# A graph network on one core: another form of the segment maximum, and the dense node blocks dealt to other stages

## The chip, the core and the metric

The kernel runs on one core of a Trainium2 chip. The time is device microseconds (us) of that core for one execution, median of several runs. The core has a matrix engine (TensorE, PE in the profile; its weight loads are PEld), a vector engine (VectorE, DVE), a scalar engine for functions of one input (ScalarE, ACT), a general engine (GpSimd, POOL) which here issues the indirect DMAs (gathers and scatters of rows by an index list), and SyncE (SP), which issues the plain DMAs. Each engine runs its own program in order; they meet at semaphores.

## The reference

100,000 nodes with 64 features, 25,000 edges sorted by their target `dst`. Four graph layers follow each other, each as `x = layernorm(x + layer(x))`. Cut to what matters:

```python
# layer 0
logits  = w1[target] - w2[source] + d            # per edge, 64 channels
seg_max = segment_max(logits, target)
e       = exp(logits - seg_max[target])
a       = e / segment_sum(e, target)[target]
out     = segment_sum(a * (w3[source] + d), target)
# layer 1: mean of neighbours, two products, batch norm, relu, row normalisation
# layer 2: attention with one head (leaky relu, segment softmax)
# layer 3: three graph convolutions, the last one into a softmax
h = relu(conv(x, W1, b1)); h = relu(conv(h, W2, b2)); h = conv(h, W3, b3)
x = layernorm(x + softmax(h, axis=1))
```

A node that is no edge's target gets nothing from segment sums, so its row goes through all four layers alone ("dense" work). Rows of nodes with edges are computed apart and written over the dense ones at the end.

## The kernel before

Edges are handled in 25 steps (`ITERS`) of two chunks (b = 0, 1) of 512 edges. A chunk lies with 64 or 128 channels on the partitions and 512 edges along the free axis, so that sums and maxima over the edges of one target are scans along that axis: `k.same` holds 1 where an edge has the target of the edge before it. The program is a row of stages, each with a barrier at its end: index work; an edge network; the first attention (`attention_stage`); the mean layer; batch norm; the update; the dense stage; the second attention; the convolutions `gcn1_stage`, `gcn2_stage`; the output stage. Tiles are named by stage (`at_`, `me_`, `up_`, `de_`, `g_` for both convolutions, `ou_`).

**The dense work** is cut into 97 blocks of 1024 nodes (8 nodes on each of 128 partitions) and a last one of the same size that overlaps (98 blocks). `DenseLane` holds the instructions of a block, as three parts that are pipelined: x (batch norm product up to `dve_norm2`), y (the three products of layer 3, `pe_turn3` to `pe_zback`) and z (softmax and layer norm, `dve_max` to `dve_norm4`, then a store to `out`). A stage that takes blocks along runs, at edge step q, part x of its block q, part y of block q-1 and part z of block q-2 between its own instructions; `LaneOrder` holds that order. The order on each engine is written by hand in the function `step` of each engine's block. 23 blocks lie in gcn1, 22 in gcn2, 23 in the output stage and 30 in the dense stage, where two lanes run side by side (15 pairs).

**The first attention** needs the running maximum of the logits over the edges of a target. ACT makes `anew` (0 where the edge continues its target, -1e30 where it starts a new one). DVE scans with state = max(state + anew, logit) into M (L1215), and later makes L = logit - M (L1239), A = M of the edge before + anew (L1240) and A = A - M (L1243): the exponents of the edge's weight and of the decay of the running sum. ACT takes their exponentials (L1149, L1140), and DVE's next step scans the sums (L1180, L1184). In the same ACT program, between them, stand `act_flat` (L931) and the squares of the finished rows, L1137, on which DVE's L1247 waits.

**Gathers** are issued by POOL in `gather_loop` (L1346): eight indirect DMAs of 128 rows a step (sixteen in the first attention), and a copy of the next index columns (L1331, L450). W has two buffers, so POOL may be two steps ahead of the transposes that free them.

**The output stage** has two parts. In 25 steps it gathers, scans and keeps the third convolution of all edges in `G3` in SBUF, with 23 blocks beside it. Then each engine runs `finish` 25 times: softmax, residual and layer norm of one step's edges (DVE L3352 to L3383, ACT L3288 to L3298), into a buffer F, and POOL scatters F into `out` with eight indirect DMAs a step (`scatter`, L3117). The scatter waits (`beside.stored`) until all blocks are stored, since it writes over their rows. F has two buffers; L3383 waits until the scatter of two steps before has landed. The loads of the residual rows (`rest`, X3) are issued by SP after all block loads.

## Time and profile before

| | us |
|---|---|
| median of 3 runs (3369.0 to 3388.23) | 3370.6 |
| profiled execution, its own time | 3347.96 |
| span of the profiled execution | 3346.2 |
| first attention, 240 to 876 | 636 |
| gcn1, 1962 to 2330 | 368 |
| gcn2, 2332 to 2757 | 425 |
| output stage, steps with gathers, 2759 to 3062 | 303 |
| output stage, finish and scatter, 3062 to 3346 | 284 |

The page gives each engine's busy time over the whole span; since the stages have different limits, the shares of the stages decide. The PEclk slices are tenths of TensorE's full clock; the last three of the forty are 5, with PE idle. "Idle before" of a row names what ended the wait of the instruction.

### The profile page before, as it was taken

To read this page: it belongs to the slowest core of one execution; us is meant where nothing else is said; L and a number is where in the kernel's file an instruction comes from. 1 tells how busy PE (TensorE), PEld (TensorE's weight loads), DVE (VectorE), ACT (ScalarE), POOL (GpSimd) and SP (SyncE) were. 2 spreads that over 40 slices of the span, in tenths; PEclk is the share of its full clock that TensorE was granted. 3 is DMA by queue.
4 is the path that set the end of the run, shared out by engine and by line. 5 is a ranking of instruction groups with operands and counts; after the bars stand their busy time and mean duration, and the time that the engine had idled before them with its cause. 6 is when DMAs were issued, how large, how long until landed. Compare 5 with 4: busy or idle time off the path is not lost. (4 is left out here: it accounts for less than half of the span.)

```text
span 3346.2 us, 53978 instructions
## 1 busy us (share of the span) xinstructions
PE 2459.9 (74%) x14171; PEld 1675.7 (50%) x14171; DVE 2486.4 (74%) x4558; ACT 1724.2 (52%) x3950; POOL 1925.5 (58%) x1870
## 2 busy tenths in 40 slices
PE   3976666666578789979946779998999998995000
PEld 1543444444467667745525556665666656663000
DVE  5569999999777758859966747776566665888553
ACT  3784444444222258858841126665566655775221
POOL 4008888887488800068870047775655437886776
PEclk9988787787777888879977989998999998997555
DMA  4133333433466668733313445555445543332111
GB/s 129 64 96 87 107 99 107 109 106 98 119 199 196 191 144 180 153 104 115 112 46 75 113 127 167 157 162 159 135 136 141 139 106 108 112 114 68 47 47 27
DMA packets 742887, 393.28 MB, mean 118 GB/s; under 512 B 517090, under 2 KB 649265, under 8 KB 742770
## 3 DMA queue, kind: packets, MB, share of 16 engines
q1 hardware_dynamic: 691582, 333.94, 36.4%
q0 software_dynamic: 51200, 58.03, 6.8%
q8 instruction: 54, 0.88, 0.1%
q14 instruction: 51, 0.42, 0.0%
HBM read 217.18 MB, written 175.64 MB: 117 GB/s over the span
## 5 line engine op out<-in xcount | busy, mean ns | idle before, releaser
L1341 POOL DMA_INDIRECT g_W<-t,g_cols x400 | 463.2, 1158 | 260.8 <-PE g_pS L2901 116.4
L460 POOL DMA_INDIRECT fr_W<-in_x,fr_idx x400 | 496.0, 1240 | 127.6 <-issue 107.7
L1341 POOL DMA_INDIRECT me_W<-t,me_cols x200 | 236.0, 1180 | 58.0 <-issue 46.9
L1341 POOL DMA_INDIRECT ou_W<-t,ou_cols x200 | 222.6, 1113 | 58.1 <-issue 40.8
L3433 POOL DMA_INDIRECT de_V<-t,de_cols x200 | 215.8, 1079 | 53.6 <-issue 41.4
L3117 POOL DMA_INDIRECT out<-ou_F,ou_ways x200 | 200.1, 1000 | 77.5 <-issue 53.3
L1058 PE MATMUL at_pL<-at_XF,w_logit 128*128 128x512 f32 x100 | 89.7, 996 | 123.0 <-ACT at_XF L1105 123.0
L1331 POOL COPY g_cols<-pos 128x8 int32 (+1 forms) x50 | 19.8, 396 | 241.2 <-POOLq L85 241.0
L1331 POOL COPY de_cols<-pos 128x8 int32 (+1 forms) x25 | 8.1, 324 | 261.4 <-POOLq L85 261.2
L931 ACT ACTIVATE me_nzt<-me_pXT 128x512 f32<-128x512 f32 x47 | 28.1, 598 | 170.9 <-PE me_pXT L914 170.9
L914 PE MATMUL at_pXT<-ident,at_nz 128*128 128x128 f32 x200 | 40.3, 336 | 93.8 <-ACT at_nzt L931 52.3
L1887 DVE TENSOR_TENSOR_SCAN me_S<-same,me_S,me_pA 64x512 f32<-64x512 f32 (+1 forms) x50 | 63.6, 1271 | 58.9 <-issue 40.1
L1058 PEld LDWEIGHTS at_pL<-at_XF,w_logit 128*128 128x128 f32 x100 | 28.3, 313 | 154.4 <-ACT at_XF L1105 129.6
L450 POOL COPY fr_idx<-src 128x8 int32 (+1 forms) x25 | 6.9, 278 | 160.1 <-POOLq L85 159.8
L3383 DVE TENSOR_TENSOR ou_F<-ou_O,ou_st 128x256 f32<-128x256 f32 x50 | 21.1, 425 | 96.8 <-DMA out<-ou_F,ou_ways 83.0
L3288 ACT ACTIVATE ou_O<-ou_O 128x256 f32<-128x256 f32 x50 | 18.8, 418 | 142.4 <-DVE ou_O L3359 142.4
L1490 DVE TENSOR_TENSOR g_T<-g_pY,g_st 128x512 f32<-128x512 f32 x45 | 30.8, 684 | 82.3 <-PE g_pY L1471 82.3
L1563 PE MATMUL g_pH<-g_H,w 128*128 128x512 f32 x180 | 88.1, 612 | 0.0
L2444 ACT ACTIVATE a_QY<-a_pB 128x512 f32<-128x512 f32 x25 | 14.9, 598 | 140.1 <-PE a_pB L2421 140.1
L3030 DVE TENSOR_TENSOR_SCAN g_S<-same,g_S,g_WF 128x512 f32<-128x512 f32 (+1 forms) x50 | 64.3, 1286 | 28.8 <-ACT g_WF L2961 28.8
L2419 PE MATMUL a_pB<-center,a_S 64*128 64x64 f32 x400 | 56.1, 281 | 38.5 <-DVE a_S L2546 38.3
L2116 PE MATMUL up_pU<-center,up_U 128*128 128x128 f32 x400 | 66.8, 336 | 15.5 <-DVE up_st L2222 15.5
(619 smaller groups left out, 8536.8 us busy)
## 6 DMA issues: line engine op xcount, KB each, us to landing
mg_y<-wanted SPq DMA_DIRECT2D x50, 256.0 KB
at_nx<-in_x SPq DMA_DIRECT2D x50, 256.0 KB, 2.6
x<-at_nz SPq DMA_DIRECT2D x50, 256.0 KB, 3.3
x1T<-at_nzt SPq DMA_DIRECT2D x50, 256.0 KB, 2.9
t<-up_X SPq DMA_DIRECT2D x100, 128.0 KB, 2.0
t<-g_HS SPq DMA_DIRECT2D x50, 256.0 KB
t<-g_HD SPq DMA_DIRECT2D x50, 256.0 KB, 3.4
g_D<-t SPq DMA_DIRECT2D x50, 256.0 KB
```

Of the source, the lines that this page charges most:

```text
L460: self.nc.gpsimd.indirect_dma_start(out=self.W[w][b][:, (2 * t + h) * C:(2 * t + h + 1) * C], out_offset=None, in_=self.table, in_offset=b ...
L914: s = self.nc.tensor.transpose(self.pXT[:, n * P:n * P + P], self.Z[b][:, n * (P + 1):n * (P + 1) + P], self.k.ident[:, :])
L1058: t.matmul(pL[b][:, :], k.w_logit[:, :], XF[b][:, :], start=True, stop=False, skip_group_check=True)
L1341: nc.gpsimd.indirect_dma_start(out=slot(w, b, t), out_offset=None, in_=table, in_offset=bass.IndirectOffsetOnAxis(ap=cols[w][:, c:c + 1], ...
L1490: self.nc.vector.tensor_tensor(groups(self.T[:, :], G), groups(self.pY[:, :], G), over(self.st[:, 1, :], C), ALU.mult).then_inc(e["scaled" ...
L1563: s = self.nc.tensor.matmul(self.pH[:, h, :], self.k.w2[:, :], self.H1[:, h, :], start=True, stop=True)
L1887: v.tensor_tensor_scan(S[b][:, :], k.same[0:C, at], pA[b][:, :], S[1 - b][:, CE - 1:CE], ALU.mult, ALU.add).then_inc(e["summed"], 1)
L2116: i = t.matmul(pU[x % 2][b][:, n * P:n * P + P], U[x % 2][b][:, n * P:n * P + P], k.center[:, :], start=True, stop=True)
L2419: t.matmul(pB[w][:, m:m + C], S[b][:, n * P:n * P + P], k.center[0:C, 0:C], start=b == 0 and n == 0, stop=False, skip_group_check=True)
L3030: v.tensor_tensor_scan(S[b][:, :], k.same[:, at], WF[b][:, :], S[1 - b][:, CE - 1:CE], ALU.mult, ALU.add).then_inc(e["summed"], 1)
L3117: nc.gpsimd.indirect_dma_start(out=out, out_offset=bass.IndirectOffsetOnAxis(ap=ways[w][:, c:c + 1], axis=0), in_=F[w][b][:, t * C:(t + 1) ...
L3433: nc.gpsimd.indirect_dma_start(out=V[h][:, t * C:t * C + C], out_offset=None, in_=k.t2, in_offset=bass.IndirectOffsetOnAxis(ap=cols[w][:, ...
```

## The change

Three things change (`update_stage` is the same in both).

1. **First attention.** `same` is read one edge ahead (it has two more columns, zeros), and the scan is state = max(state, logit) + anew of the next edge. M then holds the running maximum before an edge (or about -1e30 where the edge starts a target). DVE makes A = M of the edge before - logit in one subtraction per chunk, directly after the scans. ACT makes L = relu(A) and A = relu(-A), and takes exp(-L) and exp(-A). These four ACT instructions stand behind `act_flat` and ahead of the squares L1137.
2. **Blocks.** gcn1 takes 21 blocks, gcn2 none, the output stage 47, the dense stage 30 as before. gcn2's own instructions keep their order.
3. **Output stage.** Its 25 steps with gathers take blocks 0 to 24 of its 47; the finish steps take the others along: function `late` holds, for each engine, part x, y and z of the lane interleaved with the finish of edge step f. DVE writes the finished rows back into `G3`; POOL copies them into F (two copies of 128x256 a step), loads a number from a table `needed`, waits until that many blocks are stored, and scatters. The table is made at the start from the last target of each step (one DMA of 25 numbers, eight small DVE instructions). `rest` loads are interleaved with the block loads.

```diff
-BLOCKS_G1, BLOCKS_G2, BLOCKS_OU = 23, 22, 23
-BLOCKS_BESIDE = BLOCKS_G1 + BLOCKS_G2 + BLOCKS_OU
+BLOCKS_G1, BLOCKS_OU = 21, 47
+FIRST_OU = D_FULL - BLOCKS_OU
+FIRST_G1 = FIRST_OU - BLOCKS_G1
...
-                        reuse(act, e["diffs"], 2 * q)
-                        s.activation(anew[b][:, :], k.same[:, bass.ds((2 * q + b) * CE, CE)], ACT.Copy,
+                        reuse(act, e["maxed"], 2 * q)
+                        s.activation(anew[b][:, :], k.same[:, bass.ds((2 * q + b) * CE + 1, CE)], ACT.Copy,
...
+                        act.wait_ge(e["diffs"], last_of(q, b))
+                        s.activation(L[b][:, :], A[b][:, :], ACT.Relu).then_inc(e["bent"], 1)
+                        s.activation(A[b][:, :], A[b][:, :], ACT.Relu, scale=-1.0).then_inc(e["bent"], 1)
...
-                        act.wait_ge(e["diffs"], last_of(q, b))
-                        s.activation(A[b][:, :], A[b][:, :], ACT.Exp).then_inc(e["decay"], 1)
+                        act.wait_ge(e["bent"], 4 * q + (2 * b + 2))
+                        s.activation(A[b][:, :], A[b][:, :], ACT.Exp, scale=-1.0).then_inc(e["decay"], 1)
...
-                        v.tensor_tensor_scan(M[b][:, 1:CE + 1], anew[b][:, :], pL[b][:, :], M[1 - b][:, CE:CE + 1],
-                                             ALU.add, ALU.max).then_inc(e["maxed"], 1)
+                        v.tensor_tensor_scan(M[b][:, 1:CE + 1], pL[b][:, :], anew[b][:, :], M[1 - b][:, CE:CE + 1],
+                                             ALU.max, ALU.add).then_inc(e["maxed"], 1)
                         dve.wait_ge(e["maxed"], last_of(q, b))
+                    for b in first:
+                        v.tensor_tensor(A[b][:, :], M[b][:, 0:CE], pL[b][:, :], ALU.subtract)\
+                            .then_inc(e["diffs"], 1)
...
-                    for b in first:
-                        v.tensor_tensor(L[b][:, :], pL[b][:, :], M[b][:, 1:CE + 1], ALU.subtract)
-                        v.tensor_tensor(A[b][:, :], M[b][:, 0:CE], anew[b][:, :], ALU.add).then_inc(e["shifted"], 1)
-                    for b in first:
-                        dve.wait_ge(e["shifted"], last_of(q, b))
-                        v.tensor_tensor(A[b][:, :], A[b][:, :], M[b][:, 1:CE + 1], ALU.subtract)\
-                            .then_inc(e["diffs"], 1)
                     for b in second:
...
+class LateOrder(LaneOrder):
+
+
+    def run_late(self, eng, step, late):
+
+        last = 2 * ITERS
+        assert ITERS % 2 == 1 and self.count % 2 == 1 and ITERS + 4 < self.count < last - 1
+        for q in range(3):
+            step(q, q % 2, *self.of(q))
+        with eng.Fori(0, (ITERS - 3) // 2) as j:
+            step(2 * j + 3, 1, 2 * j + 3, 2 * j + 2, 2 * j + 1)
+            step(2 * j + 4, 0, 2 * j + 4, 2 * j + 3, 2 * j + 2)
+        for q in range(ITERS, ITERS + 2):
+            late(q - ITERS, q % 2, *self.of(q))
+        with eng.Fori(0, (self.count - ITERS - 2) // 2) as j:
+            late(2 * j + 2, 1, 2 * j + (ITERS + 2), 2 * j + (ITERS + 1), 2 * j + ITERS)
+            late(2 * j + 3, 0, 2 * j + (ITERS + 3), 2 * j + (ITERS + 2), 2 * j + (ITERS + 1))
+        for q in range(self.count, last):
+            late(q - ITERS, q % 2, *self.of(q))
...
+                        if again(q):
+                            pool.wait_ge(scattered[w][b], ring_count(q, w, 16 * CT) - 16 * CT)
+                        nc.gpsimd.tensor_copy(F[w][b][:, :], G3[:, bass.ds((2 * q + b) * (CT * C), CT * C)])\
+                            .then_inc(copied, 1)
+                    blocks = nc.gpsimd.value_load(needed[0:1, bass.ds(q, 1)], min_val=16, max_val=16 * BLOCKS_OU)
+                    pool.wait_ge(lane.o_out, blocks)
+                    for b in range(2):
+                        pool.wait_ge(copied, last_of(q, b))
...
-                beside.stored(pool)
+                pool.wait_ge(told, 8)
...
+                def late(f, w, x, y, z):
+                    if x is not None:
+                        lane.pe_product(pe, x, w, None)
+                    if y is not None:
+                        lane.pe_turn3(pe, y, 1 - w)
+                    if x is not None:
+                        lane.pe_sums(pe, x)
+                    if y is not None:
+                        lane.pe_first(pe, y)
+                    if x is not None:
+                        lane.pe_upright(pe, x)
+                    if y is not None:
+                        lane.pe_second(pe, y)
+                        lane.pe_third(pe, y)
+                        lane.pe_zback(pe, y)
+
+                beside.run_late(pe, step, late)
...
+                def late(f, w, x, y, z):
+                    if x is not None:
+                        lane.act_relu(act, x)
+                        lane.act_square(act, x)
+                    if y is not None:
+                        lane.act_flat3(act, y)
+                    if z is not None:
+                        lane.act_exp(act, z)
+                    soft(f)
+                    if y is not None:
+                        lane.act_hidden(act, y)
+                    if x is not None:
+                        lane.act_log(act, x)
+                        lane.act_inverse(act, x)
+                    if z is not None:
+                        lane.act_square4(act, z)
+                    if y is not None:
+                        lane.act_deeper(act, y)
+                    if x is not None:
+                        lane.act_square2(act, x)
+                    squares(f)
+                    if y is not None:
+                        lane.act_zflat(act, y)
+                    if z is not None:
+                        lane.act_log4(act, z)
+                        lane.act_dev4(act, z)
+                    if x is not None:
+                        lane.act_log2(act, x)
+                        lane.act_dev2(act, x)
+                    spread(f)
+
+                beside.run_late(act, step, late)
...
+                def norm(f):
+                    for b in range(2):
+                        dve.wait_ge(e["dev"], last_of(f, b))
+                        v.tensor_tensor(part(f, b), O4(b), over(st[b][:, 4, :], C), ALU.mult).then_inc(e["norm"], 1)
...
+                def late(f, w, x, y, z):
+                    if z is not None:
+                        lane.dve_max(dve, z)
+                        lane.dve_less(dve, z)
+                    top(f)
+                    if x is not None:
+                        lane.dve_clamp(dve, x)
+                    by_degree(f)
+                    if z is not None:
+                        lane.dve_esum(dve, z)
+                        lane.dve_recip(dve, z)
+                        lane.dve_soft(dve, z)
+                        lane.dve_mix4(dve, z, w)
+                    total(f)
+                    if x is not None:
+                        lane.dve_scale(dve, x)
+                        lane.dve_mix2(dve, x, w)
+                    mix(f, 1 - w)
+                    if z is not None:
+                        lane.dve_sumsq4(dve, z)
+                    if x is not None:
+                        lane.dve_sumsq2(dve, x)
+                    if z is not None:
+                        lane.dve_norm4(dve, z)
+                    sumsq(f)
+                    if x is not None:
+                        lane.dve_norm2(dve, x, w)
+                    norm(f)
...
+                dve.wait_ge(ends_in, 16)
+                v.tensor_scalar(share[:, :], ends_of[:, :], 1.0 / DN, None, ALU.mult).then_inc(told, 1)
+                dve.wait_ge(told, 1)
...
+                dve.wait_ge(told, 7)
+                v.tensor_copy(needed[:, :], whole[:, :]).then_inc(told, 1)
...
+                beside.run_late(dve, step, late)
...
-        pairs = (D_FULL + 1 - BLOCKS_BESIDE) // 2
-        assert (D_FULL + 1 - BLOCKS_BESIDE) % 2 == 0 and pairs % 2 == 1
+        pairs = (FIRST_G1 + 1) // 2
+        assert (FIRST_G1 + 1) % 2 == 0 and pairs % 2 == 1
```

In gcn2 each engine's `step(q, w, x, y, z)` becomes `step(q, w)` with the same own calls and no lane call.

What the change does to the order on ACT in one steady step of the first attention (XF the gathered rows, nzt the transposed rows of the node lane, R the squares L1137, zt the small statistics). Before:

```order
L887 ACTIVATE at_nst<-at_nst,eps 128x8 x2
L892 ACTIVATE at_nst<-at_nst 128x8 x2
L931 ACTIVATE at_nzt<-at_pXT 128x512
L1137 ACTIVATE at_R<-at_Z 128x256 x2
L1140 ACTIVATE at_A<-at_A 128x512 x2
L1143 ACTIVATE at_zt<-at_zt,eps 128x4 x2
L1147 ACTIVATE at_zt<-at_zt 128x4 x2
L1149 ACTIVATE at_L<-at_L 128x512 x2
```

The same stretch of ACT with the change:

```order
L889 ACTIVATE at_nst<-at_nst,eps 128x8 x2
L894 ACTIVATE at_nst<-at_nst 128x8 x2
L933 ACTIVATE at_nzt<-at_pXT 128x512
L1138 ACTIVATE at_L<-at_A 128x512
L1139 ACTIVATE at_A<-at_A 128x512
L1138 ACTIVATE at_L<-at_A 128x512
L1139 ACTIVATE at_A<-at_A 128x512
L1143 ACTIVATE at_R<-at_Z 128x256 x2
L1146 ACTIVATE at_A<-at_A 128x512 x2
L1149 ACTIVATE at_zt<-at_zt,eps 128x4 x2
L1153 ACTIVATE at_zt<-at_zt 128x4 x2
L1155 ACTIVATE at_L<-at_L 128x512 x2
```

Four wide instructions now stand ahead of the squares `at_R`.

On DVE in a finish step of the output stage, before (G the kept sums, O and Q work tiles of the edges, st their statistics):

```order
L3352 TENSOR_REDUCE ou_st<-ou_G 128x4 x2
L3356 TENSOR_TENSOR ou_O<-ou_G,ou_st 128x256 x2
L3359 TENSOR_TENSOR ou_O<-ou_O,dinv 128x256 x2
L3363 TENSOR_REDUCE ou_st<-ou_O 128x4 x2
L3366 RECIPROCAL ou_st<-ou_st 128x4 x2
L3369 TENSOR_TENSOR ou_O<-ou_O,ou_st 128x256 x2
L3373 SCALAR_TENSOR_TENSOR ou_O<-ou_O,ou_X 128x256 x2
L3377 TENSOR_REDUCE ou_st<-ou_Q 128x4 x2
L3383 TENSOR_TENSOR ou_F<-ou_O,ou_st 128x256 x2
```

The second half of such a step with the change, with lane instructions (L1492 to L1667) between:

```order
L3407 TENSOR_REDUCE ou_st<-ou_O 128x4 x2
L3410 RECIPROCAL ou_st<-ou_st 128x4 x2
L1492 TENSOR_TENSOR ou_T<-ou_pY,ou_st 128x512
L1499 TENSOR_TENSOR ou_Y<-ou_T,ou_X_7 128x512
L3415 TENSOR_TENSOR ou_O<-ou_O,ou_st 128x256 x2
L3419 SCALAR_TENSOR_TENSOR ou_O<-ou_O,ou_X 128x256 x2
L1649 TENSOR_REDUCE ou_st<-ou_Q 128x8
L1511 TENSOR_REDUCE ou_st<-ou_R 128x8
L1667 TENSOR_TENSOR ou_O<-ou_E,ou_st 128x512
L3425 TENSOR_REDUCE ou_st<-ou_Q 128x4 x2
L1531 TENSOR_TENSOR ou_X_7<-ou_Y,ou_st 128x512
L3431 TENSOR_TENSOR ou_G<-ou_O,ou_st 128x256 x2
```

The last one writes G, no longer F. POOL in the last scatter step with the change (before it was the DMAs and the copy of `ou_ways` alone):

```order
L3092 COPY ou_F<-ou_G 128x256 x2
L3094 TENSOR_LOAD ou_needed
L3094 ISA x2
L3101 DMA out<-ou_F,ou_ways 100000x64 x8
```

Two copies, a load of a register and its wait now stand ahead of each step's eight DMAs.

## Rows read from the trace of the kernel before

**Rows 1.** Busy time by stage: first attention, mean, dense, gcn1, gcn2, output, finish.

```profile
core 0: us, PE busy (x) PEld busy (x) DVE busy (x) ACT busy (x) POOL busy (x), PEclk, DMA share, GB/s
240.00:876.00 636.00, 400.86 (x1802) 264.91 (x1802) 619.96 (x1122) 300.53 (x801) 472.17 (x414) 0.79 0.37 102
876.00:1189.00 313.00, 234.09 (x1474) 201.29 (x1474) 231.96 (x354) 74.13 (x192) 241.23 (x225) 0.77 0.64 182
...
1440.00:1753.00 313.00, 252.45 (x1144) 139.95 (x1144) 249.41 (x440) 216.60 (x451) 248.72 (x274) 0.88 0.30 95
...
1962.00:2330.00 368.00, 353.38 (x2124) 242.76 (x2124) 260.04 (x399) 225.30 (x445) 263.04 (x224) 0.94 0.57 157
2332.00:2757.00 425.00, 413.26 (x2286) 263.86 (x2286) 268.59 (x436) 254.95 (x530) 218.90 (x224) 0.98 0.49 135
2759.00:3062.00 303.00, 276.89 (x1666) 186.05 (x1666) 233.44 (x351) 218.09 (x444) 232.89 (x225) 0.94 0.36 104
3062.00:3346.00 284.00, 1.51 (x10) 1.23 (x9) 149.14 (x451) 59.53 (x203) 208.25 (x224) 0.50 0.17 44
```

**Rows 2.** Timeline, first attention, one step: start, duration, engine, line, tiles, count, [idle before].

```profile
526.33 1.27 DVE L1215 TENSOR_TENSOR_SCAN at_M<-at_anew,at_M,at_pL 128x512 f32<-128x512 f32 x1
...
529.40 0.58 ACT L931 ACTIVATE at_nzt<-at_pXT 128x512 f32<-128x512 f32 x1
...
531.27 0.75 ACT L1137 ACTIVATE at_R<-at_Z 128x256 f32<-128x256 f32 x2 [1.29 <-DVE at_Z L1236]
...
531.49 0.68 DVE L1239 TENSOR_TENSOR at_L<-at_pL,at_M 128x512 f32<-128x512 f32 x1
...
533.89 1.29 DVE L1243 TENSOR_TENSOR at_A<-at_A,at_M 128x512 f32<-128x512 f32 x2
...
534.05 2.00 POOL L460 DMA_INDIRECT fr_W<-in_x,fr_idx  x1 [0.30 <-issue]
...
534.61 1.23 ACT L1140 ACTIVATE at_A<-at_A 128x512 f32<-128x512 f32 x2 [2.59 <-DVE at_A L1243]
...
535.09 0.74 DVE L1247 TENSOR_REDUCE at_zt<-at_R 128x4 f32<-128x256 f32 x2
```

**Rows 3.** Timeline of POOL: index copies, one per step of gathers (attention, gcn2).

```profile
337.03 1.69 POOL L450 COPY fr_idx<-src 128x8 int32 x1
...
365.72 0.46 POOL L450 COPY fr_idx<-src 128x8 int32 x1
...
2370.49 0.20 POOL L1331 COPY g_cols<-pos 128x8 int32 x1
...
2381.84 0.20 POOL L1331 COPY g_cols<-pos 128x8 int32 x1
```

**Rows 4.** Timeline of DVE in gcn2: the first scan of each of the last two steps.

```profile
2734.69 1.28 DVE L3030 TENSOR_TENSOR_SCAN g_S<-same,g_S,g_WF 128x512 f32<-128x512 bf16 x1 [0.49 <-ACT g_WF L2961]
...
2745.70 1.28 DVE L3030 TENSOR_TENSOR_SCAN g_S<-same,g_S,g_WF 128x512 f32<-128x512 bf16 x1
```

**Rows 5.** Groups by line (output stage; gcn1): busy, mean ns | idle before.

```profile
L3320 DVE TENSOR_TENSOR_SCAN ou_T<-same,ou_T,ou_pA 64x512 f32<-64x512 f32 (+1 forms) x42 | 53.1, 1264 | 3.1 <-PE ou_pA L3197 3.1
...
L1341 POOL DMA_INDIRECT g_W<-t,g_cols x200 | 249.5, 1247 | 79.2 <-issue 51.3 <-PE g_pA L2659 21.6 <-POOL g_cols L1331 4.7
```

**Rows 6.** Groups by line, finish and scatter, 3062 to 3346.

```profile
L3117 POOL DMA_INDIRECT out<-ou_F,ou_ways x200 | 200.1, 1000 | 77.5 <-issue 53.3 <-DVE ou_F L3383 20.2 <-POOL ou_ways L1331 3.9
L3383 DVE TENSOR_TENSOR ou_F<-ou_O,ou_st 128x256 f32<-128x256 f32 x50 | 21.1, 425 | 96.8 <-DMA out<-ou_F,ou_ways 83.0 <-ACT ou_st L3298 13.7
```

**Rows 7.** Timeline, finish: last norm, last scatter; and landing of scatters.

```profile
3316.25 0.42 DVE L3383 TENSOR_TENSOR ou_F<-ou_O,ou_st 128x256 f32<-128x256 f32 x1 [3.85 <-DMA out<-ou_F,ou_ways]
...
3334.69 0.98 POOL L3117 DMA_INDIRECT out<-ou_F,ou_ways  x1 [0.30 <-issue]
...
DMA to landing us min/median/max: 2.1/2.2/3.0
```

**Rows 8.** Timeline of POOL, dense stage: a copy of the size of F.

```profile
1558.63 0.53 POOL L3425 COPY rows<-de_V 128x256 f32 x1
```

More of the change, by code:

```diff
@@ L2871, in step @@
                         own_rows(q + 2, w)
-                    beside.load(sp, q + 2, w)
                     store(q)
-                    beside.store(sp, q - 2, out)
                 for q in range(2):
                     own_rows(q, q, used=False)
-                    beside.load(sp, q, q)
-                beside.run_queue(sp, step)
-                beside.stored(sp)
+                with sp.Fori(0, ITERS // 2 - 1) as j:
+                    step(2 * j, 0)
+                    step(2 * j + 1, 1)
+                for q in range(ITERS - 3, ITERS):
+                    step(q, q % 2)
                 for b in range(2):
@@ L2942, in step @@
                     second_d(q, w, 1)
-                    if y is not None:
-                        lane.pe_third(pe, y)
                     third(q, 0, HD, pD, "relu_d", "third_d")
                     third(q, 1, HD, pD, "relu_d", "third_d")
-                    if y is not None:
-                        lane.pe_zback(pe, y)
-                beside.run(pe, step)
+                by_ring(pe, step)
             @block.scalar
@@ L3171, in step, with late @@
                     beside.store(sp, q - 2, out)
+                def late(q, w, f):
+                    beside.load(sp, q + 2, w)
+                    if not isinstance(f, int) or f + 2 < ITERS:
+                        rest(f + 2, 1 - w)
+                    beside.store(sp, q - 2, out)
+                sp.dma_start(ends_of[:, :], a["dstp"][BEFORE:BEFORE + EP].rearrange("(a q e) -> a q e", a=1, q=ITERS)
+                             [:, :, 2 * CE - 1], allow_slow_non_contiguous=True).then_inc(ends_in, 16)
+                rest(0, 0)
+                rest(1, 1)
                 for q in range(2):
@@ L3176, in _ @@
                     beside.load(sp, q, q)
-                beside.run_queue(sp, step)
-                rest(0, 0)
-                rest(1, 1)
-                with sp.Fori(0, ITERS // 2 - 1) as j:
-                    rest(2 * j + 2, 0)
-                    rest(2 * j + 3, 1)
-                rest(ITERS - 1, 0)
+                beside.queue_late(sp, step, late)
+                beside.stored(sp)
             @block.tensor
```

198 lines of the change are left out of this document (81 added, 117 removed).

## The prediction

> **What bounds the kernel now.** I read the busy time by stage first [rows 1], because the change gives to one stage what it takes from another, and then, in each stage touched, the engine that never waits. In the first attention DVE is busy 620 of 636 us, with ACT at 301: DVE is the bound. In gcn1 and gcn2 it is PE, busy 353 of 368 and 413 of 425 us. In the output stage's steps with gathers POOL is busy 233 us and needs some 0.3 us between two issues, 60 us for 200 of them, so 293 of 303: POOL is the bound, with PE, DVE and ACT close below. In finish and scatter PE does nothing, DVE is busy 149 of 284 us, and POOL sets the pace: 277.6 us of issues and waits before them, of which 20 are the first wait, and 8 of copies, 10.6 us a step [rows 6]. DVE waits 83 us there for scatters to land, so that is where work could be put for nothing, up to POOL's pace.
>
> **First attention.** DVE loses L1239 and L1240, two each a step: four instructions that start at 531.49 and end at 533.89, 2.40 us; and two L1243, 533.89 to 535.09, 1.20 us [rows 2]. It gains two subtractions of the same shape, 1.20. The scan keeps its shape, 1.27. Net 2.40 us a step, 60 us in 25 steps, if nothing fills the hole. ACT gains four instructions of 128x512; a pair takes 1.23 [rows 2], so 2.4 us a step. What hid ACT was DVE's 3.6 us of L1239 to L1243: the squares L1137 were made while they ran, and L1247 waits for those squares. Now the four new ones stand ahead of the squares. Counted from the scan at 526.33: the subtractions push the node lane's work 1.2 us back, so `act_flat`, which ended at 529.98, ends near 531.2; four instructions to 533.5; first square done at 533.9. DVE gets to L1247 at 535.09 - 2.4 = 532.7 and stands 1.2 us. A little more (0.2) is lost at the last norm, which waits on ACT again. So a step saves 2.4 - 1.4 = 1.0 us: **24 us of the 60**. POOL agrees with that size: it issues sixteen gathers a step all through, and gains about 1 us, since the issue that took 2.00 us beside L1243 [rows 2] loses that neighbour.
>
> **gcn1.** Two blocks fewer. A step is 368/25 = 14.7 us; without a lane it falls to POOL's pace (below), 12. Two steps: **-5 us**.
>
> **gcn2.** All 22 blocks leave. What is left of PE's work is shown by the last step but one, which has no lane work on PE but the last of part z on DVE: 2734.69 to 2745.70, 11.0 us [rows 4]. POOL, where it isn't held by PE, took 2370.49 to 2381.84 = 11.35 us a step [rows 3]; the mean stage, alike in its gathers and without blocks, needs 313 us for 25 steps, 12.5 with its ends [rows 1]. I take 11.7 a step: 10.7 us before the first scan, 24 x 11.7 = 281, and 11.3 us from the last step's scan to the end (2745.7 to 2757): 303 us. **-122 us**. Bounds: 11.35 a step gives -130; the mean stage's 313 us gives -112.
>
> **Output stage, steps with gathers.** POOL's pace is the same. The last two steps now have full lane work: **+3 us**.
>
> **Late steps.** Each of the 25 finish steps now has DVE's finish work, 149.14/25 = 6.0 us, and for 22 of them a whole block: in the steps before, DVE is busy 233.44 us, less 50 scans of 1.264 [rows 5], over 23 blocks = 7.4 us. Sum 13.4 us, over POOL's old 10.6, so DVE takes over. Stalls: I laid one late step out from the rows' durations; DVE stands once, at the lane's last norm, which waits for ACT's `squares`, `zflat` and two small ones in a row behind DVE's `mixed`: 0.5 us with PE at 2.4 GHz. PE's lane work is 252.45/30 = 8.4 us a block at a granted clock of 0.88 (dense stage), 7.4 at full, just over half of 14. The first attention, with PE at 401 us of 636 and 0.79, full-clock work of one half too, says that the clock granted will be near 0.8, between its two levels (1.2 and 2.4 GHz); the two products and their evictions then end about 0.6 later. So 14.5 us a step: 22 x 14.5 = 319, and 34.5 for the last three, with less lane work (13, 11.5, 10): 353.5. Bounds of a step: 13.5 (no clock loss), 16.2 (PE at 1.2 GHz throughout, 14.8 us of work and the chain through it).
>
> POOL in a late step: 10.6, two copies of 0.53 [rows 8], and the register load, which the trace does not show: at least nothing, at most a trip to memory and back like a DMA's landing, 2.2 us [rows 7]; I take 1.0, nearer the middle. That is 12.7, under 14.5, so it hides, if its issues stay at 1.0 us each. By the Trainium skill (DMA: Bandwidth & Descriptors, section Latency and other measured facts) a `tensor_load` has a floor of some 600 ns; the POOL step would be 12.3.
>
> The end: in the kernel before, the last norm was at 3316.25 and the last scatter's issue at 3334.69 [rows 7]; POOL was behind. Now POOL waits for the last norm: copies and load 2.0, eight issues 10.3, landing 2.2, and what followed the landing, 3346.2 - 3337.9 = 8.3: 22.8 us. The first finish instruction was at 3062.8. So the new end, on the old clock: 3062.8 + 3 + 353.5 + 22.8 = 3442, **+96 us** against 3346.
>
> The small table at the start of the stage (one DMA, eight instructions of 25 numbers on DVE) runs while the first gathers fly, 10 us; it costs nothing, and 2 us if it didn't. SP's `rest` loads wait for `mixed` of the step, ahead of the store of part z: the store is issued after that anyway.
>
> **Sum:** -24 - 5 - 122 + 96 = **-55 us**. Of the profiled execution, 3347.96, that makes 3293. The median of the runs shown is 3370.6, 22.6 above the profiled one; I put the change to it: **3316 us**, 1.6% less.
>
> **Rivals.**
> A. *ACT does not hold DVE in the attention* (its stretch before L1137 has 1.3 us idle [rows 2]; the shift may be absorbed). Then the full 60: 3280 us. Against: the order of the four instructions ahead of the squares is fixed. 0.15.
> B. *gcn2 stays bound by PE.* With a sixth less to do, the granted clock may sink from 0.98 to the mean stage's 0.77 [rows 1]. If all of the 11.0 us went with the clock it would be 11.0 x 0.98/0.77 = 14.0; some two thirds do, since the scan and the evictions between do not: 12.9 in place of 11.7, +29, 3345 us. Against: gcn2's own work fills most of 11.7 us. 0.12.
> C. *POOL becomes the bound of the late steps by waits on DVE.* In gcn1 the gathers took 1.247 us each [rows 5], against 1.000 in the finish. With 1.25: 8 x 0.25 more, 14.7, and copies at 0.9 and dearer load make 15.6. First norm near 3080, 25 x 15.6, end 10.5: 3480, 38 us over my sum, 3354 us. 0.13. The Trainium skill (SBUF — State Buffer, section SBUF: two separate sides) says that DVE with two SBUF inputs and a GpSimd instruction that reads SBUF lock each other out for the whole instruction, and that descriptors issued by GpSimd wait too. The 2.00 us issue beside L1243 agrees; by that rule the two F copies could also hold DVE, 1.1 us a late step, which would end near the same 3340.
> D. *Slower: the same, worse.* The attention has steps in which sixteen issues took 365.72 - 337.03 = 28.7 us [rows 3], 14.3 for eight. With copies and load of 3.8 that is 18.1 us a late step: 25 x 18.1 = 452, end 3543 on the old clock, +197 in place of +96: 46 us slower than before, 3417 us. It decides from 16.3 us a step on, where the gain of the other stages is used up. Against: such steps ended after the first five; in the finish POOL had 1.000 each with DVE at 53%. For: DVE will be at 93%. 0.08.
> E. *The pieces do not add up as written* (for instance the scatter waits for blocks that are stored late: but step f needs about 4f - 45 blocks and f + 24 are stored). 0.02.
>
> **Numbers.** My case 0.50, A 0.15, B 0.12, C 0.13, D 0.08, E 0.02. Together with a late step of 13.5 and A the low end is 3316 - 36 - 8 = 3272; the high end takes in C with part of B: 3366. Under 1% either way can't be told from no change. Faster by more: my case nearly whole, A, and a little of B and C: 0.68. Slower by more: D and half of E: 0.09. The rest 0.23.
>
> **What would show it.** Attention 636 to about 612, with DVE idle before the reduction of the squares, released by ACT; if it is near 576, A. gcn2 near 303 with POOL's issues back to back; PE's clock of 0.8 and a longer stage is B. Late steps of 14.5 with DVE busy over 90% and POOL waiting on its norm; POOL without waits and issues over 1.2 us is C or D. The forecast fails if DVE's idle share in the late steps is over 15%: then a wait I did not lay out (ACT's order, the store of O, the loads) is there.

## The result, and the profile after

The changed kernel takes **3271.1 us** (median of 4 runs, 3256.6 to 3286.9), where the kernel before took 3371.8 in the same comparison (3369.0 to 3388.2): a ratio of 0.9689, interval 0.9655 to 0.9723. That is 101 us less, 3.1%; in a second comparison it was 0.9679 (0.9620 to 0.9738). Forecast were 55 us less and 3316, with a range that began at 3272: the time lies just under it. The profiled execution took 3267.9 us, its span 3266.1.

The busy time by stage of the changed kernel, with the columns of [rows 1]; its rows are the first attention, mean, dense, gcn1, gcn2, the output stage's steps with gathers, and the late steps.

```profile
core 0: us, PE busy (x) PEld busy (x) DVE busy (x) ACT busy (x) POOL busy (x), PEclk, DMA share, GB/s
251.00:853.00 602.00, 412.31 (x1802) 286.03 (x1802) 562.10 (x1022) 343.86 (x902) 440.08 (x414) 0.78 0.40 107
853.00:1164.00 311.00, 234.57 (x1474) 201.57 (x1474) 230.89 (x349) 73.86 (x192) 242.12 (x225) 0.77 0.65 184
1415.00:1733.00 318.00, 266.10 (x1144) 149.86 (x1144) 249.60 (x438) 216.50 (x452) 249.43 (x274) 0.84 0.29 94
1954.00:2305.00 351.00, 334.28 (x2048) 232.34 (x2048) 246.01 (x375) 212.00 (x417) 265.74 (x226) 0.95 0.58 161
2305.00:2596.00 291.00, 254.87 (x1450) 174.65 (x1450) 118.13 (x151) 108.33 (x201) 218.74 (x224) 0.96 0.53 137
2598.00:2903.00 305.00, 282.00 (x1722) 187.53 (x1723) 239.80 (x368) 225.46 (x459) 229.69 (x225) 0.97 0.39 112
2903.00:3266.00 363.00, 217.40 (x865) 110.91 (x864) 311.28 (x754) 228.84 (x548) 232.13 (x274) 0.85 0.27 79
```

DVE's idle time in the attention went from 16 to 40 us, and its busy time fell by 58. In gcn2, DVE's and ACT's work halved and PE lost 158 of 413 us. The late steps have DVE at 86%, with their end, and at 93% in the steady ones (278.68 of 300 us from 2920 to 3220); over 90% was forecast, and the sign of failure, over 15% idle, did not appear. The windows are rounded; the table below measures each stage from one fixed DVE instruction to the next (us), in six executions: the first profiles of both kernels, a second profile of each (E7 and E9), and E1 and E2, which are told below.

| stage | before | before, 2nd | after | after, 2nd | E1 scan | E2 blocks |
|---|---|---|---|---|---|---|
| edge network | 240.8 | 256.2 | 251.3 | 240.3 | 254.2 | 242.9 |
| first attention | 636.8 | 636.7 | 601.8 | 601.7 | 601.6 | 636.6 |
| mean to dense | 878.0 | 879.4 | 882.8 | 873.6 | 879.7 | 881.8 |
| second attention | 223.5 | 239.2 | 237.0 | 247.4 | 251.7 | 233.5 |
| gcn1 | 363.6 | 364.1 | 341.2 | 351.5 | 360.3 | 349.4 |
| gcn2 | 426.1 | 426.2 | 295.3 | 297.7 | 426.9 | 298.2 |
| output, gathers | 294.1 | 294.1 | 296.5 | 296.5 | 291.9 | 295.9 |
| late steps | 283.3 | 283.4 | 360.1 | 360.1 | 281.4 | 360.4 |
| span | 3346.2 | 3379.3 | 3266.1 | 3268.8 | 3347.5 | 3298.7 |

The stages that the change touches give, from the first trace of before to the first of after, -35.0 - 22.4 - 130.8 + 2.4 + 76.8 = -109 us. The other stages took 29 us back in that pair of traces, so the spans differ by only 80; the two medians, over more executions, by 101. What the other stages do is told with E7 and E8.

**One step of the attention**, timeline of the changed kernel (columns as in [rows 2]):

```profile
546.02 1.28 DVE L1221 TENSOR_TENSOR_SCAN at_M<-at_pL,at_M,at_anew 128x512 f32<-128x512 f32 x1
...
547.33 1.29 DVE L1225 TENSOR_TENSOR at_A<-at_M,at_pL 128x512 f32<-128x512 f32 x2
...
550.29 0.58 ACT L933 ACTIVATE at_nzt<-at_pXT 128x512 f32<-128x512 f32 x1
...
550.77 0.62 ACT L1138 ACTIVATE at_L<-at_A 128x512 f32<-128x512 f32 x1
...
551.29 0.62 ACT L1139 ACTIVATE at_A<-at_A 128x512 f32<-128x512 f32 x1
...
552.85 0.71 ACT L1143 ACTIVATE at_R<-at_Z 128x256 f32<-128x256 f32 x2
...
553.28 0.75 DVE L1249 TENSOR_REDUCE at_zt<-at_R 128x4 f32<-128x256 f32 x2 [0.82 <-ACT at_R L1143]
```

The scan starts 7.26 us before the reduction of the squares; before, it was 526.33 to 535.09, 8.76. DVE lost 2.40 us of work in a step and stands 0.82 for the squares, which ACT makes only after its four relus (550.77 to 552.9). DVE's list of waits over the stage's steps has this one row:

```profile
DVE at_zt L1249 <- ACT at_R L1143: 18.9, 23, 0.8
```

23 times, 18.9 us in all. Before there was one wait of 0.2 us.

**gcn2** is POOL's now: the index copies stand 11.2 and 11.0 us apart, and over 250 us of steady steps POOL was busy 199.0 and idle 52.0, nearly all of it the 0.3 us between two issues. PE's granted clock stayed at 0.96. Timeline, and the groups of POOL from 2330 to 2580:

```profile
2376.82 0.19 POOL L1333 COPY g_cols<-pos 128x8 int32 x1
2388.00 0.20 POOL L1333 COPY g_cols<-pos 128x8 int32 x1
2398.98 0.20 POOL L1333 COPY g_cols<-pos 128x8 int32 x1
```

```profile
L1343 POOL DMA_INDIRECT g_W<-t,g_cols x181 | 191.2, 1056 | 52.0 <-issue 45.1 <-POOL g_cols L1333 3.6 <-PE g_pS L2939 3.0
L1333 POOL COPY g_cols<-pos 128x8 int32 (+1 forms) x22 | 7.8, 355 | 0.1
```

**One late step**, timeline of the changed kernel; lines 1466 to 1667 are the lane's, from 3092 on the finish's:

```profile
3040.24 0.74 POOL L3092 COPY ou_F<-ou_G 128x256 f32 x2 [0.99 <-DVE ou_G L3431]
...
3041.93 0.98 POOL L3101 DMA_INDIRECT out<-ou_F,ou_ways  x1 [0.96 <-POOL ou_F L3092]
...
3042.88 0.16 DVE L1466 TENSOR_SCALAR ou_st<-ou_pY 128x8 f32<-128x8 f32 x1
...
3049.57 0.71 ACT L3298 ACTIVATE ou_Q<-ou_O 128x256 f32<-128x256 f32 x2
...
3050.92 0.29 ACT L1656 ACTIVATE ou_st<-ou_st,eps 128x8 f32<-128x8 f32 x1
...
3051.24 0.21 ACT L1661 ACTIVATE ou_st<-ou_st 128x8 f32<-128x8 f32 x1
...
3051.58 0.69 DVE L1667 TENSOR_TENSOR ou_O<-ou_E,ou_st 128x512 f32<-128x512 f32 x1 [0.86 <-ACT ou_st L1661]
...
3053.44 0.75 DVE L3431 TENSOR_TENSOR ou_G<-ou_O,ou_st 128x256 f32 x2
3054.11 0.74 POOL L3092 COPY ou_F<-ou_G 128x256 f32 x2 [1.82 <-DVE ou_G L3431]
...
3056.75 0.16 DVE L1466 TENSOR_SCALAR ou_st<-ou_pY 128x8 f32<-128x8 f32 x1
```

3042.88 to 3056.75 is one step: 13.87 us (13.62 in the mean of 21). DVE stands once, 0.86 us at the lane's last norm, the stall that was laid out at 0.5 and 0.6. The step before it took 13.42 us, with a stall of 0.39; the two differ in TensorE's granted clock, 1.00 and 0.88 (columns as in [rows 1]):

```profile
3029.46:3042.88 13.42, 8.36 (x40) 4.25 (x38) 12.86 (x32) 9.76 (x23) 9.47 (x12) 1.00 0.33 95
3042.88:3056.75 13.87, 10.30 (x42) 5.30 (x38) 12.84 (x32) 9.71 (x23) 9.09 (x12) 0.88 0.31 93
```

Of 21 such steps, eight had a clock of 1.00 and a stall of 0.30 to 0.39, and thirteen one of 0.87 or 0.88 and a stall of 0.39 to 0.91, 0.73 in the mean. Over all of them it is 0.60. POOL waits for DVE's `G` in turn (0.99, 1.82), copies it in 0.74 and issues its first scatter 0.96 after that, with the register load between; so the load costs at most 0.96 - 0.30 = 0.66 us. The Trainium skill (DMA: Bandwidth & Descriptors, section Latency and other measured facts) gives some 600 ns for it: the trace agrees. The groups of this stage, and its end:

```profile
L3101 POOL DMA_INDIRECT out<-ou_F,ou_ways x200 | 208.1, 1041 | 75.6 <-issue 51.8 <-POOL ou_F L3092 20.1 <-POOL ou_ways L1333 3.6
L3092 POOL COPY ou_F<-ou_G 128x256 f32 (+1 forms) x50 | 18.9, 407 | 62.2 <-DVE ou_G L3431 62.2
...
L1667 DVE TENSOR_TENSOR ou_O<-ou_E,ou_st 128x512 f32<-128x512 f32 x25 | 17.3, 692 | 18.6 <-ACT ou_st L1661 18.6
```

```profile
3237.75 0.76 DVE L3431 TENSOR_TENSOR ou_G<-ou_O,ou_st 128x256 f32<-128x256 f32 x2 [0.46 <-ACT ou_st L3307]
...
3254.49 0.98 POOL L3101 DMA_INDIRECT out<-ou_F,ou_ways  x1 [0.30 <-issue]
```

Against [rows 6], an issue takes 1.041 us in place of 1.000, and POOL has 62 us to spare (32 of them before its first copy). DVE's 83 us of waiting for scatters are gone.

### The profile page after: what moved, and what is told of

Same layout as the page of the kernel before. It is cut to its first block and busy times, and to the rows that moved or that the text cites. A ratio compares the mean times of both kernels' runs of the same rounds, so it can differ in the third digit from the quotient of the medians.

```text
span 3266.1 us, 54405 instructions
## 1 busy us (share of the span) xinstructions
PE 2558.3 (78%) x14171; PEld 1738.5 (53%) x14171; DVE 2434.4 (75%) x4466; ACT 1781.0 (55%) x4050; POOL 1916.2 (59%) x1922
## 5 line engine op out<-in xcount | busy, mean ns | idle before, releaser
L462 POOL DMA_INDIRECT fr_W<-in_x,fr_idx x400 | 460.7, 1152 | 128.8 <-issue 109.7
L1343 POOL DMA_INDIRECT g_W<-t,g_cols x400 | 456.2, 1141 | 124.8 <-issue 99.4
L3101 POOL DMA_INDIRECT out<-ou_F,ou_ways x200 | 208.1, 1041 | 75.6 <-issue 51.8
L1333 POOL COPY g_cols<-pos 128x8 int32 (+1 forms) x50 | 28.3, 566 | 250.8 <-POOLq L86 250.6
L3035 DVE TENSOR_TENSOR g_Z<-g_pD,dinv 128x256 f32<-128x256 f32 x50 | 21.2, 425 | 135.0 <-PE g_pD L2954 129.8
L1060 PE MATMUL at_pL<-at_XF,w_logit 128*128 128x512 f32 x100 | 75.7, 849 | 55.6 <-ACT at_XF L1107 55.6
L1565 PE MATMUL ou_pH<-ou_H,w 128*128 128x512 f32 x188 | 103.1, 674 | 13.6 <-ACT ou_H L1559 10.5
L916 PEld LDWEIGHTS at_pXT<-ident,at_nz 128*128 128x128 f32 x200 | 29.2, 183 | 126.5 <-issue 72.5
L924 PE MATMUL at_pG<-at_nz 128*128 128x129 f32 x400 | 82.1, 374 | 0.0
L924 PEld LDWEIGHTS at_pG<-at_nz 128*128 128x128 f32 x400 | 77.5, 287 | 0.0
```

The source lines that it names most:

```text
L462: self.nc.gpsimd.indirect_dma_start(out=self.W[w][b][:, (2 * t + h) * C:(2 * t + h + 1) * C], out_offset=None, in_=self.table, in_offset=b ...
L916: s = self.nc.tensor.transpose(self.pXT[:, n * P:n * P + P], self.Z[b][:, n * (P + 1):n * (P + 1) + P], self.k.ident[:, :])
L924: s = self.nc.tensor.matmul(pG, rows[:, 0:P], rows, start=False, stop=False, skip_group_check=True)
L1060: t.matmul(pL[b][:, :], k.w_logit[:, :], XF[b][:, :], start=True, stop=False, skip_group_check=True)
L1343: nc.gpsimd.indirect_dma_start(out=slot(w, b, t), out_offset=None, in_=table, in_offset=bass.IndirectOffsetOnAxis(ap=cols[w][:, c:c + 1], ...
L1565: s = self.nc.tensor.matmul(self.pH[:, h, :], self.k.w2[:, :], self.H1[:, h, :], start=True, stop=True)
```

## The experiments

Each of those that were timed stood against the kernel before on its own chip, whose median was 3373 to 3375 us. An edit is shown against the kernel that its heading names.

**E1, the scan's new form alone.** Kernel before, with the attention of the changed one:

```
-v.tensor_tensor_scan(M, anew, pL, carry, ALU.add, ALU.max)
+v.tensor_tensor_scan(M, pL, anew, carry, ALU.max, ALU.add)
-v.tensor_tensor(L, pL, M[1:], ALU.subtract); v.tensor_tensor(A, M[:CE], anew, ALU.add)
-v.tensor_tensor(A, A, M[1:], ALU.subtract)
+v.tensor_tensor(A, M[:CE], pL, ALU.subtract)      # ahead of lane.dve_sumsq
+s.activation(L, A, ACT.Relu); s.activation(A, A, ACT.Relu, scale=-1.0)
```

> The kernel before with only the new form of the maximum in the first attention. Theory P (as predicted): the four new ACT instructions ahead of the squares give DVE a wait of 1.2 us a step and a second small one, so the stage is 24 us shorter than before. Theory Q (from the trace of the changed kernel): ACT reaches the squares 0.4 us earlier than laid out and the second wait does not exist, 1.5 us a step, 35 us. Theory A (no wait at all): 60 us. In all: 3348 (P), 3337 (Q), 3312 us (A).

Measured: 3333.8 us (3305.2 to 3349.3), ratio 0.9869 (0.9825 to 0.9912). The attention took 601.6 us, as in the changed kernel, 35 us less, which is theory Q. The later stages kept their lengths within 3.3 us; the edge network (254.2) and the second attention (251.7) came out long, at low clocks, and what that says is told with E7 and E8.

**E2, the blocks alone.** Kernel before, with the stages from gcn1 on as in the changed one; E1's edit is left out:

```
-BLOCKS_G1, BLOCKS_G2, BLOCKS_OU = 23, 22, 23
+BLOCKS_G1, BLOCKS_OU = 21, 47
-beside.run(dve, step); by_two(dve, finish)
+beside.run_late(dve, step, late)
```

> The kernel before with only the blocks dealt anew and the late steps. As predicted, gcn1 -5, gcn2 -122, output stage +96: 31 us less, 3341 us. Theory Q (trace of the changed kernel): gcn1 -22, gcn2 -131, output stage +79: 74 us less, 3298 us. If the two parts of the change don't hinder each other, this saving and that of the scan alone add up to the whole, 100 us.

Measured: 3323.6 us (3300.4 to 3327.1), ratio 0.9874 (0.9825 to 0.9924). gcn1 349.4, gcn2 298.2, late steps 360.4: the lengths of the changed kernel. The total settles less than the stages do: 51 us less (26 to 59 by the interval) takes in the forecast's 31 and leaves out theory Q's 74, but the stages from gcn1 on are 63 us shorter than in the first trace of before, with gcn1 at -14 and not -22. In their sum the two parts don't hinder one another: their medians give -41 and -51, 92 of the 101 us, and the two ratios multiplied, 0.9745, lie within the errors of 0.969.

**E3, the relus earlier on ACT.** Changed kernel; if the relus' place makes DVE stand, another place ends it:

```
+for b in first:  act.wait_ge(diffs); Relu -> L; Relu(-x) -> A
 if q is not None: lane.act_dev(act, q)
 if r is not None: lane.act_flat(act, r, 0)
-for b in first:  act.wait_ge(diffs); Relu -> L; Relu(-x) -> A
 for b in second: act.wait_ge(zcen); Square -> R
```

> The changed kernel with ACT's four relu instructions of the first attention moved ahead of the node lane's small statistics (act_dev), into the 4 us in which ACT waits there. Theory ACT: DVE's wait of 0.8 us a step for the squares (18.9 us in 23 steps) goes, a step falls from 23.4 to 22.5 us, the whole by 20 us, 3251 us. Theory POOL: POOL issues sixteen gathers a step nearly without a pause and becomes the bound near 23 us; then less than 8 us are won.

Measured: 3261.1 us (3226.4 to 3269.4), ratio 0.9652 (0.9577 to 0.9727). The attention took 585.0, 16.8 less than in the changed kernel; the wait for the squares is gone. The whole shows 10 us less than the changed kernel's median, on another chip and with intervals that overlap, so the stage carries this reading. DVE's waits over the stage, in one row, and POOL's gathers in this kernel:

```profile
DVE at_Z L1258 <- ACT at_zt L1153: 0.5, 1, 0.5
```

```profile
L462 POOL DMA_INDIRECT fr_W<-in_x,fr_idx x348 | 388.5, 1116 | 102.9 <-issue 102.1 <-DMA fr_W<-in_x,fr_idx 0.6 <-POOL fr_idx L453 0.2
```

So the stall was real and cost what its wait shows (18.9 us against 16.8). Of 540 us POOL is now busy or between issues 500: the next bound is 1.7 us a step away (40 us over 23 steps).

**E4, 23 and 45 blocks.** Changed kernel, two blocks given back to gcn1:

```
-BLOCKS_G1, BLOCKS_OU = 21, 47
+BLOCKS_G1, BLOCKS_OU = 23, 45
```

> The changed kernel with 23 blocks in gcn1 and 45 in the output stage (21 and 47). Theory 'gathers ahead': gcn1's steps without a lane take only PE's own 8.6 to 9.8 us, since POOL is two steps ahead by then, not POOL's pace of 12; two blocks cost 10 us there, and up to 22 us with the gaps of 3 us seen before the change; the late steps lose 2 x 3 us. Net 4 to 16 us slower than the changed kernel, gcn1 351 to 363 or more. Theory as predicted: 2.5 us a block in gcn1, 3 us a block less in the late steps: no difference.

Measured: 3292.1 us (3276.8 to 3300.8), ratio 0.9762 (0.9705 to 0.9818). gcn1 took 358.2 us, 7 to 17 more; the late steps 356.2, only 4.0 less. Two blocks cost gcn1 more than they cost the late steps, so by the stages 21 and 47 is the better of the two splits. The total is 21 us above the changed kernel's, more than the 4 to 16 expected, but the two intervals overlap. Other splits weren't run.

**E5, both orders.** E3's kernel, and on DVE, in the late step, the finish's reduction ahead of the norm that stands waiting:

```
+sumsq(f)
 if z is not None: lane.dve_norm4(dve, z)
-sumsq(f)
```

> The changed kernel with the relus moved ahead as in the run before and, in the late steps, DVE's reduction of the edges' squares (sumsq) moved ahead of the lane's last norm, for which DVE waits 0.86 us on ACT. Theory DVE: the late steps are bound by DVE, a step falls from 13.65 to 12.8 us, 22 of them by 19 us: the stretch from the first finish instruction to the end from 360 to 341 us, in all 3243 us. Theory POOL: POOL's own 12.2 to 12.7 us a step and its lag let less through, under 8 us.

Measured: 3245.5 us (3226.4 to 3259.1), ratio 0.9642 (0.9609 to 0.9674). The late steps took 347.6, 12.5 less than the changed kernel's: between theory DVE (19) and theory POOL (under 8). The groups of POOL and DVE's wait, in this stage of E5:

```profile
L3101 POOL DMA_INDIRECT out<-ou_F,ou_ways x200 | 231.8, 1159 | 66.0 <-issue 57.0 <-DMA out<-ou_O 4.8 <-POOL ou_ways L1333 3.6
L3092 POOL COPY ou_F<-ou_G 128x256 f32 (+1 forms) x50 | 20.7, 449 | 34.2 <-DVE ou_G L3431 34.2
```

```profile
DVE ou_O L1667 <- ACT ou_st L1661: 3.7, 6, 1.2
```

The norm's wait fell from 18.6 us to 3.7. All waits of DVE in the stage fell from 20.0 to 7.9 us, 12.1 of the 12.5 that the stage lost. POOL, past its first 31.9, waits 2.3 for DVE in all: its issues grew from 1.041 to 1.159 us, 17 of them to over 2. A clean step is 12.91 us, from start to start of L1466:

```profile
2969.70 0.16 DVE L1466 TENSOR_SCALAR ou_st<-ou_pY 128x8 f32<-128x8 f32 x1
...
2978.69 0.68 DVE L1531 TENSOR_TENSOR ou_X<-ou_Y,ou_st 128x512 f32<-128x512 f32 x1
2978.77 2.13 POOL L3101 DMA_INDIRECT out<-ou_F,ou_ways  x1 [0.31 <-issue]
...
2982.61 0.16 DVE L1466 TENSOR_SCALAR ou_st<-ou_pY 128x8 f32<-128x8 f32 x1
```

The issue that takes 2.13 us runs beside L1531 and L3431, which read two operands in SBUF, and so do all 17 long ones; in the changed kernel POOL mostly stands waiting for `G` there. In four steps of 13.43 us the two copies of F meet DVE's L3396, which also reads two:

```profile
3086.20 1.14 DVE L3396 TENSOR_TENSOR ou_O<-ou_G,ou_st 128x256 f32<-128x256 f32 x2
3086.43 1.16 POOL L3092 COPY ou_F<-ou_G 128x256 f32 x2
```

L3396 takes 0.75 us in the other steps and the copies 0.74 in the step above, so both take some 0.4 longer where they meet. The Trainium skill (SBUF — State Buffer, section SBUF: two separate sides) says that such a DVE instruction and a GpSimd instruction that reads SBUF lock each other out; the copies agree in kind. Its sentence on DMA descriptors that GpSimd cannot write speaks of another kind of DVE instruction, a 2-port perf mode. So the doubled issue is read from the trace alone, and no run here isolates its cause. DVE remains the bound: it is busy 283.8 of 290 us in the steady steps, and none of its waits in this stage is put down to POOL. A step fell from 13.62 to 13.18 us in the mean, 0.44; theory DVE had taken the 0.86 us of one step for all, where the mean wait was 0.60. POOL stands right behind: with 4.8 us of its own waiting for stores and 2.3 for DVE it has little left.

**E6, the scatters wait for all blocks.** Changed kernel, the table of needed blocks unused:

```
-blocks = nc.gpsimd.value_load(needed[0:1, bass.ds(q, 1)], ...)
-pool.wait_ge(lane.o_out, blocks)
+pool.wait_ge(lane.o_out, 16 * BLOCKS_OU)
```

> The changed kernel with the scatters waiting until all 47 blocks are stored, as the kernel before did with its 23, in place of the wait for the number from the table. Theory: POOL then starts when the last block lands, near the end of the late steps, and scatters for 25 x 10.7 = 267 us; it saves the 22 us of scatter after the last norm: the whole 230 to 250 us longer, near 3510 us. Rival: the scatters were late anyway (waiting for stores); then little changes.

Measured, one run: 3536.4 us; the late stage took 621.9 us, 262 more, a little over the 230 to 250 expected.

```profile
POOL out L3100 <- DMA out<-ou_O: 314.0, 1, 314.0
```

One wait of 314 us, then 295 us of scatters for the 25 steps. Rival E's mechanism has this price: the kernel would be 163 us slower than before, not 101 faster.

**E7 and E8, the unchanged stages.** The kernel before once more; and the kernel before with only the two columns that the change adds to `same`:

```
-k.same = k.sb("same", [P, EP], BF16)
+k.same = k.sb("same", [P, EP + 2], BF16)
+gp.memset(k.same[:, EP:EP + 2], 0.0)
```

> The kernel before once more, for its profile. Theory clock: the edge network (241 us to the first attention) and the second attention (224 us) were at a high granted clock (0.99 from 95 to 185 us) by chance of the execution; another execution shows 241 to 257 and 223 to 252 us. Theory layout: the two new columns of same shift all later tiles in SBUF and cost those stages 10 and 13 us; then this execution shows 241 and 224 again.

> The kernel before with only the two more columns of same and their memset, unused. Theory clock: edge stage anywhere between 241 and 257 us, with the granted clock of 95 to 185 us going along. Theory layout: 251 us or more, and the second attention 237 or more.

Measured: 3381.1 and 3359.2 us, one run each. The edge network took 240.8 us in the first trace of before, 256.2 in E7, 248.9 in E8, 251.3 and 240.3 in the two traces of the changed kernel. Its length goes with PE's granted clock, not with the kernel; 95 to 185 us, first profile of before, then E7:

```profile
95.00:185.00 90.00, 86.83 (x773) 53.19 (x773) 52.69 (x128) 72.39 (x148) 0.00 (x0) 0.99 0.22 74
```

```profile
95.00:185.00 90.00, 90.00 (x656) 52.76 (x656) 43.59 (x103) 59.54 (x122) 0.00 (x0) 0.80 0.21 62
```

The same program got through 773 matmuls in 90 us at 0.99, and 656 at 0.80. The second attention goes with the clock too: 223.5 us at 0.86 and 239.2 at 0.75 in the two traces of before, 237.0 at 0.80 and 247.4 at 0.73 in those of the changed kernel. So most of the 29 us that the untouched stages took in the first pair of traces goes with the clocks of two executions, and the columns alone (248.9 and 234.4 us in E8) cost nothing that can be seen. One thing stays open: in the eight traces with the scan's new form the second attention took 237.0 to 254.0 us (251.7 in E1), in the four with the old one 223.5 to 239.2, although its code is the same. Whether the new form moves the clock there or chance did, no run decides; that E1's median fell by 41 us (30 to 59), more than its stage's 35, speaks against a cost.

**E9 and E10, the changed kernel and E5's again, on one chip.** No edit.

> The changed kernel once more, beside the next kernel on the same chip. Both theories: 3271 us within 10; its stages as in its first trace (602 attention, 341 to 352 gcn1, 291 to 300 gcn2, 360 late steps), edge network and second attention with the granted clock of the execution.

> The kernel with both orders mended, once more, beside the changed kernel. If the stage times carry it (attention 17 us less, late steps 12 us less), it is 29 us faster than the changed kernel of the same call, 0.9%. If the lower total of its first run was the granted clock of those executions, the difference is under 10 us.

Measured: 3267.7 us (3255.8 to 3279.4), ratio 0.9679 (0.9620 to 0.9738), and 3254.7 (3231.1 to 3262.0), ratio 0.9620 (0.9558 to 0.9683). The changed kernel repeats. The two orders are 13 us below it here, neither the 29 of the stage times nor under 10, and 26 below it across the first two comparisons; the intervals overlap, but the traces agree on where it comes from: attention 585.2, late steps 349.6, 27 us together. Its two medians are the lowest of the kernels run; against the changed kernel that is not clear of the noise.

E9's trace explains why gcn1 varies. Its last step, from scan to scan of L2814, took 12.1 us at a clock of 0.50, the same step of the first trace of the changed kernel 8.6 at 0.80 (changed, then E9):

```profile
2287.40:2296.00 8.60, 8.35 (x52) 6.73 (x51) 3.93 (x4) 2.28 (x4) 0.00 (x0) 0.80 0.76 222
```

```profile
2281.00:2293.10 12.10, 12.10 (x51) 9.58 (x51) 3.96 (x5) 2.41 (x5) 0.00 (x0) 0.50 0.34 98
```

And one step in the middle took 17.2 us in place of 14.1: there PE's eight matmuls of L2708 took 2.07 us, 1.16 in other steps (windows and row of E9):

```profile
1954.00:2062.50 108.50, 107.40 (x636) 74.17 (x635) 71.26 (x109) 66.00 (x130) 85.35 (x80) 0.92 0.57 156
2061.30:2067.60 6.30, 6.30 (x22) 4.70 (x22) 4.25 (x7) 2.12 (x5) 4.67 (x6) 0.58 0.21 49
```

```profile
2061.36 2.07 PE L2708 MATMUL g_pB<-w,g_T 64*128 64x128 f32 x8
```

PE had been busy nearly without a pause (107.4 of 108.5 us), and the clock fell for some 6 us all the same. Such a step of 17.2 us stood twice in either profile of before, not at all in the first of the changed kernel and in E5's, and once in each of the other eight; each costs 3.1 us.

## Why the prediction was right or wrong

The direction was right, and so was the mechanism in each stage but gcn1, where a step without a lane was put at POOL's pace and ran at PE's. **What failed is the size of all four terms of the sum, each on the dear side, the late step most**: -24, -5, -122 and +96 were forecast, and -35, -22, -131 and +79 found in the first pair of traces; -55 against -109. By its steps:

- *First attention*, -24 against -35.0 (E1 shows it alone). The work taken off DVE was right, 2.40 us a step. The step failed at "DVE stands 1.2 us" and "a little more (0.2) at the last norm": it stands 0.82, once. The laid-out chain put `act_flat`'s end 1.2 us back, at 4.9 us after the scan; the trace has it at 4.85, but the relus begin at once, 0.1 before the eviction ends, and each takes 0.52 of ACT's time when they follow one another (they were costed at 0.6), so the squares come 0.4 earlier. The second stall doesn't exist. 0.58 x 23 = 13 us, which covers the 11 that are missing. Rival A, no stall at all, was wrong: E3 had to move the relus to get it.
- *gcn1*, -5 against -22.4, or -9 between E1 and E9, which have one slow step (17.2 us, told with E9) each. Two steps of 14.1 us went, and the last two then took 22.7 us in E9 and 18.4 in the first trace: 5.5 saved, as forecast, and 9.8. The last one alone took 12.1 at a clock of 0.50 and 8.6 at 0.80. 6.2 of the 22.4 are the two slow steps of before, and 6.1 the stage's end, from the last step's scan to gcn2's first: 24.2 us before, 18.1 in the first trace of the changed kernel, 21.3 in E9. Taking POOL's pace, 12 us, for a step without a lane was wrong: the gathers were two steps ahead, so the last steps run at PE's pace, 9.8 and 8.6 in the first trace (PE busy 18.2 of these 18.4 us). In the steps just before, with lane work on PE, the clock was 1.00 in both traces: what rival B feared for gcn2 shows here, in gcn1.
- *gcn2*, -122 against -130.8. The step takes 11.03 us, not 11.7; my bound of 11.35 came from POOL's steps beside a busy DVE [rows 3], and its issues now take 1.056 us. 0.67 x 24 = 16 less, 7 of them back at the stage's ends. POOL's issues stand back to back, as was said. Rival B was refuted here: clock 0.96.
- *Late steps and the end*, +96 against +79. A step takes 13.62 us, not 14.5. This is the largest miss, 19 us in 22 steps. "Sum 13.4" is 0.4 to 0.5 too high: without its wait the mean step is 13.0, and the clean step of E5, all DVE work and no wait, is 12.91; an instruction of 0.68 us starts 0.59 to 0.61 after its neighbour where they follow without a pause, so a stage with pauses, from which the 13.4 was read, counts more for the same work. "0.5 us with PE at 2.4 GHz" and "some 0.6 later" make 1.1, and the wait is 0.60 in the mean: at most 0.39 in the eight steps at a clock of 1.00, 0.73 in the mean of the thirteen at 0.87 or 0.88. The loss from the clock is there in kind, but smaller and not in every step: the steady steps were granted 0.90, not 0.8. The end went the other way: 28.3 us from the last norm, not 22.8, since POOL still had the scatters of the step before to issue (3237.84 to 3244.23).
- *Output stage, steps with gathers*: +3 against +2.4. *Table and rest loads at nothing*: nothing of them shows.
- *The median*: put at 22.6 above the profiled execution for both kernels. That profile of before was a lucky execution (edge network at 0.99, second attention at 0.86); the medians differ by 101 us, and the touched stages (attention, gcn1, gcn2, output with gathers, late steps), in the mean over four traces with the old blocks and seven with the new ones (for the late steps the four that have them unedited), by -35 - 15 - 129 + 4 + 77 = -98.
- *Rival C and D*: POOL's step would have been 15.6 or 18.1 us; its issues took 1.041 us and it waited 62 us for DVE. E5 shows how close it is: with 12 us less of DVE's waiting in the stage, POOL has 2.3 us of waiting for DVE left past its start.

The range failed by its own bounds too. Its low end named a late step of 13.5 together with rival A, but took off 36 and 8, where that step alone is worth 22 x 1.0 = 22 us and gcn2's bound 8 more: 3316 - 36 - 22 - 8 = 3250. That its 3272 came within 1 us of the result is luck: A's 36 us were in it, and A was wrong.

## What to carry to other kernels

A stage's pace with the bound engine's work removed is best read from its own steps without that work: gcn2's last but one took 11.01 us before, and 11.03 is the steady step of the changed kernel. Read it at either level of the clock where PE is the bound: gcn1's last step took 8.6 us at 0.80 and 12.1 at 0.50. A stall is taken in the mean of many steps, not from the one that is shown: 0.60 us against 0.86. Sum an engine's step from start to start of the same instruction in a stretch without waits, not from the busy time of a window, which came out half a microsecond in 13.4 too high. And before a gain is put to a median, compare an untouched stage in two executions of the same kernel: here it moves by 16 us with the granted clock alone.
